# The opening of a window attention: query projections ahead of key projections, and one-hot rows copied ahead of the first square root

## The reference, cut to what matters

```python
h = h + _L0_ffn_ref(_layernorm(h), ...)      # the expert outputs are added to h
h = h + _L1_attn_ref(_layernorm(h), ...)
# in _L1_attn_ref, 12 heads of 64:
q, k, v = x @ wq, x @ wk, x @ wv             # split into heads
attn = softmax((q @ k.T + einsum('bhid,ijd->bhij', q, rpk)) * HD ** -0.5)
out = attn @ v + einsum('bhij,ijd->bhid', attn, rpv)
```

## Time and profile before

| | |
|---|---|
| median of 3 runs | 1672.21 us (1671.56 to 1675.51) |
| the profiled execution's own time | 1672.95 us |
| its span in the trace | 1671.2 us |
| busy: PE, DVE, ACT, POOL | 95%, 71%, 59%, 23% |
| granted TensorE clock, mean | 0.986 |

### The profile page before, as it was taken

One profiled execution on the slowest core, in us unless ns is written; L12 is line 12 of the kernel. 1 busy time (PEld: TensorE's weight loads), 2 busy tenths in 40 slices (PEclk: granted clock), 3 DMA queues, 4 the chain that ended last, 5 costly groups with the idle time before them and its releaser, 6 DMA issues. The chain is left out here.

```text
span 1671.2 us, 31054 instructions
## 1 busy us (share of the span) xinstructions
PE 1579.9 (95%) x11573; PEld 1465.1 (88%) x11573; DVE 1179.5 (71%) x2223; ACT 983.8 (59%) x1775; POOL 388.5 (23%) x421
## 2 busy tenths in 40 slices
PE   5999999978999999999999999999999999989997
PEld 5889999977899898889888889888899989878996
DVE  4887555548776786786786776777677688576554
ACT  5542222226678578678677668767767857462331
POOL 4132565540003002110210210310300310013442
PEclk9999999998999999999999999999999999899999
DMA  9212122264101101101100110110010111091221
GB/s 273 72 45 88 54 62 60 62 151 115 46 11 40 46 11 39 46 11 25 60 12 11 30 47 20 30 46 20 30 46 11 40 50 38 20 299 56 65 61 29
DMA packets 61951, 95.10 MB, mean 57 GB/s; under 512 B 15645, under 2 KB 46512, under 8 KB 61423
## 3 DMA queue, kind: packets, MB, share of 16 engines
q1 hardware_dynamic: 52606, 72.92, 15.0%
q0 software_dynamic: 9200, 20.21, 4.1%
HBM read 72.58 MB, written 21.06 MB: 56 GB/s over the span
## 5 line engine op out<-in xcount | busy, mean ns | idle before, releaser
L2761 DVE TENSOR_REDUCE a_nmx<-a_M 125x1 f32<-125x752 f32 x256 | 240.8, 940 | 125.8 <-PE a_M L2229 125.2
L2583 ACT ACTIVATE a_Phi<-a_S 125x756 fp32r<-125x756 f32 x288 | 231.0, 802 | 159.4 <-PE a_O L2352 146.5
L2886 DVE TENSOR_TENSOR a_Plo<-a_PT,a_Phi 125x756 fp32r<-125x756 f32 x288 | 281.2, 976 | 50.8 <-ACT a_PT L2583 50.0
L2583 ACT ACTIVATE a_PT<-a_S 125x756 f32<-125x756 f32 x288 | 229.9, 798 | 0.0
L1979 POOL TENSOR_TENSOR a_qlo<-a_work,a_qhi 127x750 fp32r<-127x750 f32 x48 | 79.3, 1660 | 566.1 <-PE a_S L2333 494.3
L2333 PE MATMUL a_S<-a_qhi,a_khi 128*125 128x378 f32 x576 | 154.8, 350 | 10.1 <-issue 7.1
L2345 PE MATMUL a_O<-a_Phi,a_vhi 125*128 125x378 f32 x576 | 150.3, 342 | 1.3 <-ACT a_PT L2583 1.3
L2352 PE MATMUL a_O<-a_Plo,a_vhi 125*128 125x378 f32 x576 | 147.4, 337 | 1.0 <-DVE a_Plo L2886 0.9
L2333 PE MATMUL a_S<-a_qlo,a_khi 128*125 128x378 f32 x576 | 147.0, 336 | 0.0
L2333 PE MATMUL a_S<-a_qhi,a_klo 128*125 128x378 f32 x576 | 146.9, 336 | 0.0
L2348 PE MATMUL a_O<-a_Phi,a_vlo 125*64 125x378 f32 x576 | 146.3, 335 | 0.0
(11 more groups left out here) (457 smaller groups left out, 3190.7 us busy)
## 6 DMA issues: line engine op xcount, KB each, us to landing
a_qhi<-a_rdens SPq DMA_DIRECT2D x48, 187.5 KB, 3.3
a_wkv<-a_w4k SPq DMA_DIRECT2D x8, 768.0 KB, 5.3
a_wq<-a_w4q SPq DMA_DIRECT2D x8, 768.0 KB, 6.7
a_wkv<-a_w4v SPq DMA_DIRECT2D x8, 768.0 KB, 5.8
m_w<-in_m_w SPq DMA_DIRECT2D x8, 576.0 KB, 9.0
m_X<-m_xn SPq DMA_DIRECT2D x8, 504.0 KB
m_w<-in_m_w SPq DMA_DIRECT2D x8, 384.0 KB, 5.5
m_w_ahead<-in_m_w SPq DMA_DIRECT2D x8, 384.0 KB, 7.1
```

Source lines behind the costliest of these rows:

```text
L2583: last = nc.scalar.activation(to[:, wd % 2, :].rearrange("p (a l) -> p a l", a=2), psS[wd % 2][0:P, :, 0:HP], ACT.Exp, scale=SCALE)
L2761: v.tensor_reduce(nmx[:, u % 2, c:c + 1], bank[0:P, :, 0:376], AX.XY, ALU.max, negate=True).then_inc(sg["max_ready"], 1)
L2886: v.tensor_tensor(Plo[:, wd % 2, :], PT[:, wd % 2, :], Phi[:, wd % 2, :].bitcast(F32), ALU.subtract).then_inc(sg["exp_rest"], 1)
```

## The change

On ACT, the six one-hot copies with their wait for both tables move ahead of the wait for the variance and the root. On PE, queries 0 to 5 run ahead of keys 0 to 5, and the 16 fillers between keys 1 and 2 go. Queries 0 and 1 wait for `columns_ready` 3, keys 0 and 1 for `pairs_ready` 5 and 6, keys 2 to 5 for the `khi` and `klo` of the part two before. On ACT the copies follow the same order: queries, key 0, the last `work_rows`, keys 1 to 5. On DVE all of batch 1's moments come together after `combine(1)`, then `combine(2)`, then keys 0 to 5 without anything between them, then `combine(3)`. Other stretches keep their code.

```diff
-            def keys_part(i, half, n, woven=False):
+            def keys_part(i, half, n, woven=False, opening=False):
                 wait = waiter(pe, i)
                 if n == 0:
                     pe.wait_ge(s_wkv, 64 * i + 32 * half + 16)
                     wait("columns_ready", 3)
+                if opening:
+                    if n < 2:
+                        wait("pairs_ready", n + 5)
+                    else:
+                        wait("khi_ready", n - 1)
+                        wait("klo_ready", n - 1)
+                elif n == 0:
+                    pass
                 elif n >= 4:
...
-            def queries_part(i, half, n, woven=False):
+            def queries_part(i, half, n, woven=False, opening=False):
...
-                if n < 2 or woven:
+                if opening and n < 2:
+                    wait("columns_ready", 3)
+                elif n < 2 or woven:
...
             keep_running(7, psO[:, 1])
-            for n in range(4):
-                if n == 2:
-                    keep_running(16, psO[:, 1])
-                keys_part(0, 0, n)
             for n in range(6):
-                queries_part(0, 0, n)
-            keys_part(0, 0, 4)
-            keys_part(0, 0, 5)
+                queries_part(0, 0, n, opening=True)
+            for n in range(6):
+                keys_part(0, 0, n, opening=True)
...
         def _(act):
-            act.wait_ge(s_ln, 1)
-            nc.scalar.activation(rstd[:, 0:CH], rstd[:, 0:CH], ACT.Sqrt).then_inc(s_sd, 1)
             act.wait_ge(s_oh, 32)
             for hh in range(HG):
                 nc.scalar.activation(khi[64:128, hh, :], oh, ACT.Copy)
+            act.wait_ge(s_ln, 1)
+            nc.scalar.activation(rstd[:, 0:CH], rstd[:, 0:CH], ACT.Sqrt).then_inc(s_sd, 1)
...
-            for n in range(4):
-                keys_part(0, 0, n)
             for n in range(6):
                 queries_part(0, 0, n)
                 if n:
                     work_rows(0, 0, n - 1)
-            keys_part(0, 0, 4)
-            keys_part(0, 0, 5)
+            keys_part(0, 0, 0)
             work_rows(0, 0, HG - 1)
+            for n in range(1, 6):
+                keys_part(0, 0, n)
...
             dve.wait_ge(s_sum3, 1)
-            for n in range(4):
+            moments(CH, 2 * CH)
+            combine(2)
+            for n in range(6):
                 keys_part(0, 0, n)
-                if n < 3:
-                    moments(CH + 2 * n, CH + 2 * n + 2)
-            combine(2)
             combine(3)
-            keys_part(0, 0, 4)
-            keys_part(0, 0, 5)
```

## The result

The changed kernel takes 1677.71 us (median of 7 runs, 1676.77 to 1680.80), the kernel before 1671.56 us in the 7 runs beside it (1669.67 to 1675.51). The ratio is 1.0041 with a 95% interval of 1.0030 to 1.0052: slower by 6.15 us going by the medians, by 6.9 going by the ratio. The forecast was +5.9 us. The profiled execution took 1676.77 us.

A forecast was written before the change was run, and what follows sets the result against it. DVE was taken to bound the stretch from the bias to the first table copy. Terms of 3.3, 1.4 and 1.2 us summed to +5.9 us: 1678.9 on the profiled execution, 1678.1 against the median; range 1671.5 to 1682.5.

The forecast's parts named there:

- The one-hot landing and the root: ACT's opening: tables land at 362.7, copies end 367.1, table load 1.28 us in the open, root at 368.4, +3.0 us.
- Rival B: ACT's table load stays at the block's start, root late by 1.8 us: +4.6 us, 1676.8; chance 0.10.
- Term one: Opening up to the bias: late root +3.0, half clock in PE's fillers +1.6, slack -1.3, sum +3.3 us.
- Term two: Six key parts with nothing between: DVE waits 2.3, half clock 0.8, less former waits 1.7, sum +1.4 us.
- Term three: Table sets: PE idles over 3 us, starts set 4 at half clock, loses 1.6 us, 0.4 covered, sum +1.2 us.
- A: PE's granted clock holds through the idle stretches, so no half-clock costs: +2.3 us, 1674.5; chance 0.17.
- C: One-hot tables land by 359.7, so copies hide ahead of the root: -0.7 us, 1671.5; chance 0.13.

The follow-up runs named there:

- table early: The change plus a one-element root ahead of the wait for the one-hot tables, so ACT's table loads at the block's start; ratio 1.0028 to the kernel before.
- Copies only: The kernel before with only the six one-hot copies moved ahead of the root; ratio 1.0021 to the kernel before.
- fillers: The change with more PE fillers: 64 for 52 at the start, 14 between keys 1 and 2, 26 for 12 ahead of table set 4; ratio 1.0018.
- order and fillers: The change with the root back ahead of the one-hot copies, 14 fillers between keys 1 and 2, 26 for 12 ahead of table set 4; ratio 1.0012.
- zero rows: The change with the rows ahead of the root copied from a tile of zeros, not the loaded one-hot tables; ratio 1.0009 to the kernel before.
- copies late: The kernel before with the one-hot copies behind key parts 0 and 1 on ACT and 5 for 14 fillers ahead of the third turned group; ratio 1.0011.
- the same filled: The copies late kernel with 26 in place of 16 fillers between keys 1 and 2; ratio 1.0000 to the kernel before.

## Why the prediction held, step by step

**The one-hot landing and the root.** Forecast 362.7, seen 362.93 in the span's time. That it came so close is luck, for 362.7 was only the middle of a stretch of 8 us. The landing itself repeats: ACT's wait ended 10.1 to 10.5 us from the block's start in all five profiles that show it. The table load moved behind the sixth copy and took 1.28 us in the open; the root stood at 368.63 for a forecast of 368.4. Rival B (load at the block's start) is refuted by the row, and table early shows the load's price apart. The drain that the Trainium skill ("ScalarE: Activation LUTs", What ACT_TABLE_LOAD costs) adds is not there: the load starts where the sixth copy ends, and the root follows the load after 0.01 us.

**Term one,** +3.3 forecast: the bias is 2.9 late from the block's start (both profiles of the change), 3.3 in the span's time, of which 0.44 is the earlier stages' variation. The slack of 1.33 us and the half clock both came as costed. PE's idle stretch was 2.73 us and not 3.3, as the opening fillers started 0.44 us later and took 13.93 us in place of 13.55. Copies only and fillers give 1.3 to 1.4 for the part without the clock.

**Term two,** +1.4 forecast: 2.7 in the first profile, 1.6 in the second. The mechanism was right, and the size too small. Fillers and order and fillers show the two full-clock rounds at 2.3 us, as worked out. But the half clock lasted through both rounds, not one (their waits are 1.95 and 1.53 us); then even `klo` 3 and 5, which I had without a wait, waited 0.46 us each. My upper bound of +2.2 left these two out.

**Term three,** +1.2 forecast: from the first table copy to `qhi` 7.8 us in place of 7.3, so +0.55. PE's idle time and the half clock came (3.91 us, 0.50), but set 5 cost DVE only a wait of 0.58. The mis-sized part is PE's loss, which I put at 1.6 us. From the start of set 4 to the end of set 5 PE took 0.9 us longer than before, nearly all of it in the value product (1.96 us in place of 1.14): the two sets took 1.57 and 1.53 us at half clock, 1.52 and 1.48 at full. Set 4 also started 0.2 us sooner behind the first table copy. The cover was smaller than the 0.4 us that I read, about 0.1: the row puts the end of set 5 at 408.34, not 408.1. The term was over-sized by half.

The errors nearly cancel (-0.4, +1.3 and -0.65 us, from the block's start): `qhi` is 6.1 us late for a forecast of 5.9. That a delay of `qhi` passes on to the end holds nearly: the first exponential is 5.8 us late, the last 6.3, and from the first to the last exponential all 14 profiles took 1013.1 to 1014.0 us. That the medians, too, differ by 6.15 is in part luck, as the last stage's variation shows.

**The rivals.** A (the clock holds) is what fillers imitates: +2.1 at `qhi` for a forecast of +2.3. B is what table early builds: PE idled 2.10 us, as said, but `qhi` was 2.8 us late for a forecast of +4.6, as the clock did not fall behind that stretch. C (early tables) was to give -0.7; zero rows gave +2.2, because the clock still falls at the keys and the tables, and since the combine meets its load, of which I took no account. C's sum was too favourable, but it did not decide. The queries ahead of the keys hid behind the combines, as said.

## What to carry to other kernels

Ahead of an in-order engine's work on the path, put only what is ready by then. Six cheap copies made the bias 1.3 us late at full clock and 2.9 with its fall, because their load landed 10 us into the block and because they pushed a table load out of idle time. When independent work is bundled on the bounding engine, look at the loop that it used to be woven into: here moments had covered the round trip DVE, PE, ACT of the double-buffered key parts, and bundling them laid it bare. When filler matmuls are removed or outlasted, recount PE's idle stretches, since the half clock behind a stretch cost about as much as the stretch's own dependence: 1.6 us beside 1.3 ahead of the turned tiles, 2.1 beside 2.3 in the key waits. And the best use of DVE was the reverse of the change: keys first, while the rows are still on their way.

## What was not expected of the hardware

An idle stretch of PE of similar length was followed by half clock or not: after 2.73 us the 28 filler instructions took 4.92, after 2.51 and 2.10 us they took 3.29, and after 3.44 us the clock was down at once and the same fillers took 4.15. The same program showed two of these. Once down at the keys, the clock stayed at half for 10 us although PE was busy for a little over 7 of them, and in the second profile of the change it came back sooner.

The load of batch 1's rows, issued in the same order, was waited for until 21.4 us from the block's start in one profile (copies late) and until 22.4 in another (the same filled). And the last stage, unchanged, took between 231.6 and 236.1 us from the last exponential's end.
